# Expert weights: a casting DMA for w3, casts of w2 on ScalarE, two staging tiles for w1

## What is computed

```python
expert_weights, token_indices = jax.lax.top_k(expert_probs, cap)      # cap = 256 of 2048 tokens
expert_inputs = jax.vmap(lambda h, i: h[i])(hidden_states, token_indices)
gate = jax.nn.silu(jnp.einsum('becd,edf->becf', expert_inputs, w1))   # w1: (16, 1024, 2048) f32
value = jnp.einsum('becd,edf->becf', expert_inputs, w2)               # w2: (16, 1024, 2048) f32
expert_out = jnp.einsum('becf,efd->becd', gate * value, w3)           # w3: (16, 2048, 1024) f32
weighted = expert_out * expert_weights[..., None]                     # then scatter-added to tokens
```

## Time and profile before

| | us |
|---|---|
| median of two timed executions (6585.3 and 6603.8) | 6594.55 |
| the profiled execution, its own time | 6640.32 |
| its span on the slowest core (6) | 6638.7 |
| spans of the other cores | 6535.8 to 6595.6 |
| expert stage in it, first load to last y product | 3661 to 6111 |

### The profile page before, as it was taken

How to read it: one execution, slowest core, us unless ns; L and a number is a source line. 1 busy time by engine, 2 the same in 40 slices (tenths; PEclk the granted TensorE clock), 3 DMA queues, 4 the chain that set the end, 5 groups by cost and what they waited for, 6 DMA issues and landing times.

```text
span 6638.7 us, 53086 instructions; the slowest of 8 cores (6535.8 to 6638.7 us)
## 1 busy us (share of the span) xinstructions
PE 2939.7 (44%) x16857; PEld 1796.4 (27%) x16857; DVE 2005.4 (30%) x5175; ACT 879.9 (13%) x1731; POOL 169.8 (3%) x278
## 2 busy tenths in 40 slices
PE   0016263535353535744200455554554555455565
PEld 0004141323231323431000233433333333333222
DVE  1112131312221222224146233333333333233434
ACT  0004141415040404330000000000000000000000
POOL 0000000000000000000000000000000000000000
PEclk9977576767666766777555767777777777778888
DMA  1220101010101010013100554455565555453001
GB/s 45 58 58 4 51 4 51 5 50 6 49 5 49 5 49 5 10 62 106 38 9 1 177 167 156 152 165 163 170 177 161 174 171 168 158 165 111 32 32 35
DMA packets 387412, 541.05 MB, mean 82 GB/s; under 512 B 184100, under 2 KB 200774, under 8 KB 387142
## 3 DMA queue, kind: packets, MB, share of 16 engines
q1 hardware_dynamic: 263590, 235.36, 12.6%
q10 hardware_dynamic: 84992, 167.79, 8.1%
q0 software_dynamic: 38560, 134.51, 6.3%
HBM read 474.67 MB, written 29.36 MB: 76 GB/s over the span
## 4 chain that ended last, share of the span: by engine, by line
PE 33%; DMA 25%; DVE 17%; SPq 15%; issue 6%; DVEq 2%; ACT 2%; ACTq 0%; POOL 0%; POOLq 0%
DMA s_wf<-w 18%; SPq L85 15%; PE pO L521 8%; PE pO L1083 4%; PE pS L1165 4%; DMA s_otT<-s_otil 3%; DVEq L74 2%; PE pO L978 2%; DVE s_w3c L950 2%; PE pQ L404 2%; PE pQ L528 2%; DVE s_m L803 1%; PE pA L404 1%; PE pA L528 1%; DVE s_ohs L1153 1%
## 5 line engine op out<-in xcount | busy, mean ns | idle before, releaser
L521 PE MATMUL pO<-s_v,s_et 128*128 128x257 bf16 x4096 | 664.9, 298 | 424.5 <-ACT s_et L512 396.2
L521 PEld LDWEIGHTS pO<-s_v,s_et 128*128 128x128 bf16 x4096 | 432.1, 106 | 638.3 <-issue 517.5
L404 PE MATMUL pQ<-s_xnT,s_wqT 128*128 128x512 bf16 x256 | 80.6, 485 | 1093.9 <-DVE s_qt L412 722.7
L1054 PE MATMUL pQ<-s_xgT,s_w2c 128*128 128x256 bf16 x1024 | 224.2, 410 | 631.5 <-ACT s_gs L1047 631.5
L1083 PE MATMUL pO<-s_w3c,s_hb 128*128 128x512 bf16 x1024 | 344.1, 511 | 342.4 <-DVE s_hb L1072 342.4
L950 DVE CAST s_w3c<-s_wf 128x1024 bf16<-128x1024 f32 x256 | 177.6, 694 | 758.7 <-DMA s_wf<-w 574.8
L512 ACT ACTIVATE s_et<-pQ,s_bias 128x512 bf16<-128x512 f32 x512 | 338.5, 689 | 89.8 <-PE pQ L498 59.2
L1047 ACT ACTIVATE s_gs<-pQ 128x256 bf16<-128x256 f32 x128 | 42.2, 381 | 2289.6 <-DVE s_w2c L950 2269.2
L512 ACT ACTIVATE s_et<-pA,s_bias 128x512 bf16<-128x512 f32 x512 | 340.5, 691 | 27.6 <-PE pA L528 13.9
L404 PEld LDWEIGHTS pQ<-s_xnT,s_wqT 128*128 128x128 bf16 x256 | 29.8, 119 | 1142.1 <-issue 1132.9
L1054 PEld LDWEIGHTS pQ<-s_xgT,s_w2c 128*128 128x128 bf16 x1024 | 140.5, 142 | 704.7 <-issue 647.8
(11 more groups left out here) (198 smaller groups left out, 4065.1 us busy)
## 6 DMA issues: line engine op xcount, KB each, us to landing
s_wf<-w ACTq DMA_DIRECT2D x256, 512.0 KB, 6.0
s_wf<-w SPq DMA_DIRECT2D x256, 512.0 KB, 5.2
s_wf<-w POOLq DMA_DIRECT2D x256, 512.0 KB, 5.5
s_xstage<-x SPq DMA_DIRECT2D x16, 512.0 KB, 3.7
s_wsf<-wq ACTq DMA_DIRECT2D x16, 512.0 KB, 4.1
s_wsf<-wk ACTq DMA_DIRECT2D x16, 512.0 KB, 3.7
s_wsf<-wv ACTq DMA_DIRECT2D x16, 512.0 KB, 3.7
s_wsf<-wo ACTq DMA_DIRECT2D x16, 512.0 KB, 3.8
```

The costliest lines, as they stand in the source:

```text
L404: ins = t.matmul(bank[:], wbuf[:, j * 256 + et * 128: j * 256 + et * 128 + 128], s_xnT[:, j * T + qc * 512: j * T + (qc + 1) * 512], start ...
L521: return t.matmul(pO[qt][:, 0:257], s_et[:, kt * 512 + qt * 128: kt * 512 + qt * 128 + 128], s_v[:, kt * 257:(kt + 1) * 257], start=(kt == ...
L1054: g_ins = t.matmul(fb[f][:, 0:256], s_w2c[par][:, j * 512 + f * 128: j * 512 + f * 128 + 128], s_xgT[:, j * 256:(j + 1) * 256], start=(j = ...
```

## The change

- w3: no staging tile and no cast on an engine. One DMA from GpSimd's queue brings the chunk's 2 MB of f32 and writes bf16 straight into `s_w3c[npar]`. It waits for the y products that last read this buffer; the y products wait for it directly.
- w1: two staging tiles, `s_wf1[0]` and `s_wf1[1]`, with a semaphore each, so two quarters are loaded at a time. VectorE still casts them.
- w2: one staging tile. ScalarE both issues the loads and casts them (`AF.Copy`). The first load of the next chunk stands ahead of this chunk's silu, the four casts and the other three loads behind it.
- The first chunk is filled in the same way, w1 and w3 first, then w2.

```diff
+    s_wf1 = [sb(f"s_wf1{i}", [128, 1024], F32) for i in range(2)]
+    s_wf2 = sb("s_wf2", [128, 1024], F32)
+    ds_f1 = [p.dma_sem("ds_f1a"), p.dma_sem("ds_f1b")]
+    ds_f2 = p.dma_sem("ds_f2b")
+    ds_w3 = [p.dma_sem("ds_w3a"), p.dma_sem("ds_w3b")]
...
+    def issue_w1(e, dffc, qtr):
+        buf = qtr % 2
+        p.need("y", stg1_free[buf])
+        p.dma("y", s_wf1[buf][:].rearrange("p (j q) -> p j q", j=2),
+              wsrc(1, e, dffc, qtr), ds_f1[buf])
+
+    def cast_w1(qtr, par):
+        buf = qtr % 2
+        p.need_dma("v", ds_f1[buf])
+        p.need("v", w_cons[par][1])
+        tok = p.prod("v", lambda v, qtr=qtr, par=par, buf=buf: v.tensor_copy(
+            s_w1c[par][:, qtr * 1024:(qtr + 1) * 1024], s_wf1[buf][:]))
+        stg1_free[buf] = tok
+        wcast[par][1] = tok
...
+    def issue_w2(e, dffc, qtr):
+        p.need("s", stg2_box[0])
+        p.dma("s", s_wf2[:].rearrange("p (j q) -> p j q", j=2),
+              wsrc(2, e, dffc, qtr), ds_f2)
+
+    def cast_w2(qtr, par):
+        p.need_dma("s", ds_f2)
+        p.need("s", w_cons[par][2])
+        tok = p.prod("s", lambda s, qtr=qtr, par=par: s.activation(
+            s_w2c[par][:, qtr * 1024:(qtr + 1) * 1024], s_wf2[:], AF.Copy))
+        stg2_box[0] = tok
+        wcast[par][2] = tok
+
+    def load_w3(e, dffc, par):
+        p.need("g", w_cons[par][3])
+        p.dma("g", s_w3c[par][:].rearrange("p (q n) -> p q n", q=4),
+              w3.ap()[e][dffc * 512:(dffc + 1) * 512, :].rearrange(
+                  "(q p) n -> p q n", p=128),
+              ds_w3[par])
+
+    load_w3(0, 0, 0)
     for _q in range(4):
-        emit_casts()
-        issue_quarter(0, 0, _q, 0)
+        issue_w1(0, 0, _q)
+        cast_w1(_q, 0)
+    for _q in range(4):
+        issue_w2(0, 0, _q)
+        cast_w2(_q, 0)
...
-            emit_casts()
             if nxt is not None:
-                for qq in range(4):
-                    issue_quarter(nxt[0], nxt[1], qq, npar)
-                    emit_casts()
+                ne, nd = nxt
+                load_w3(ne, nd, npar)
+                issue_w1(ne, nd, 0)
+                issue_w1(ne, nd, 1)
+                cast_w1(0, npar)
+                issue_w1(ne, nd, 2)
+                cast_w1(1, npar)
+                issue_w1(ne, nd, 3)
+                cast_w1(2, npar)
+                cast_w1(3, npar)
+                issue_w2(ne, nd, 0)
             p.need("t", wcast[par][1])
...
                     s_gs[:, f * 256:(f + 1) * 256], fb[f][:, 0:256], AF.Silu)))
+            if nxt is not None:
+                for qq in range(4):
+                    cast_w2(qq, npar)
+                    if qq < 3:
+                        issue_w2(nxt[0], nxt[1], qq + 1)
             p.need("t", *sil)
...
             p.need("t", thb)
-            p.need("t", wcast[par][3])
+            p.need_dma("t", ds_w3[par])
```

More of the change, by code:

```diff
@@ L220, in build_program @@
     ds_smt = p.dma_sem("ds_smt")
-    ds_f = {k: p.dma_sem(f"ds_f{k}") for k in (1, 2, 3)}
     ds_wr = p.dma_sem("ds_wr")
@@ L918, in build_program @@
     prev_tym = None
[L920 to L924, removed]
-    w_cons = [{1: None, 2: None, 3: None} for _ in range(2)]
[L926 to L953, removed]
-    for _q in range(4):
-        emit_casts()
-        issue_quarter(0, 0, _q, 0)
+    s_wf1 = [sb(f"s_wf1{i}", [128, 1024], F32) for i in range(2)]
@@ new lines, in build_program, with wsrc @@
+    s_wf2 = sb("s_wf2", [128, 1024], F32)
+    ds_f1 = [p.dma_sem("ds_f1a"), p.dma_sem("ds_f1b")]
+    ds_f2 = p.dma_sem("ds_f2b")
+    ds_w3 = [p.dma_sem("ds_w3a"), p.dma_sem("ds_w3b")]
+    stg1_free = [None, None]
+    stg2_free = None
+    wcast = [{1: None, 2: None} for _ in range(2)]
+    w_cons = [{1: None, 2: None, 3: None} for _ in range(2)]
+    def wsrc(k, e, dffc, qtr):
+        w = w1 if k == 1 else w2
+        return w.ap()[e][qtr * 256:(qtr + 1) * 256,
+                         dffc * 512:(dffc + 1) * 512].rearrange(
+            "(j p) q -> p j q", p=128)
@@ new lines, in build_program @@
+    stg2_box = [None]
+    def issue_w2(e, dffc, qtr):
[15 more added lines that the diff above has]
+              ds_w3[par])
```

## The result

The changed kernel takes 6353.7 us in the median against 6614.4 for the kernel before in the same comparison; the ratio is 0.9605 (95% interval 0.9571 to 0.964). (Ratios use only executions in which neither half of the chip ran at a lower granted clock; medians are of all executions.) It is faster, by about 261 us where 421 were forecast, and 6353.7 lies 9 us above the range. A second comparison gave 0.9686 (0.964 to 0.9732).

A forecast was written before the change was run, and what follows sets the result against it. Round trips in the expert stage were taken as the bound, silu waiting for w2's cast. Saved: 402 us over 15 experts, minus 2.5 in the last, plus 22 at the start, 421; 6594.55 - 421 = 6174 us, range 6010 to 6345.

The forecast's parts named there:

- What bounds the kernel: Expert stage: round trips, not a full engine; silu waits for VectorE's w2 cast, 152.9 us an expert.
- DVE casts: VectorE keeps 4 of 12 casts per chunk: nothing by itself, w1 rounds hidden, DVE busy 354 us less.
- rival C: ScalarE reloads its function table between silu and copy: 9 us an expert, 144 in all, 6318 us; chance 0.03.
- The landing L: Time for one 512 KB w2 quarter on ScalarE's queue to land: 5.3 us, bounds for the mean 3.8 and 7.7.
- p: One w2 round on ScalarE, landing plus cast plus gaps: 6.6 us, with 1.3 for cast and gaps.
- the prediction's own form: Whole kernel, us saved = 15 x (99.4 - 11p) + (70.1 - 11p) + 22; zero at p = 9.0.
- The first interval: First to second chunk's silu in an expert, quarter 0 already landed: 2.7 + 3p = 22.5 us.
- Boundary, start and end: Silu across experts 50.8 us instead of 69.5; start saves 22 us; last expert's three intervals cost 2.5 us more.
- A: Expert stage: w2 lands in 3.8 us and the products become the bound, 685 us saved, 5909 us; chance 0.09.
- B: Loads bound by their rate, intervals inside an expert stay, only the boundary falls: 302 us saved, 6293 us; chance 0.12.
- the main case: Likeliest case for w2 quarters in the expert stage: landing between 4.3 and 6.5 us; chance 0.65.
- D: w3's 2 MB load slows w2 quarters; no gain from 7.7 us landing, 6877 us at 9.3; chance 0.05.

The follow-up runs named there:

- w2_part_only: The kernel before with only the w2 part: ScalarE issues and casts w2, w1 and w3 through VectorE as before; ratio 0.9999 to the kernel before.
- no_w3: The changed kernel with w3 loaded only for the first two chunks, later chunks using stale weights; 6110 us in the profiled execution.
- no_w1: The changed kernel with w1 loaded and cast only for the first two chunks; 6142 us in the only execution.
- all_cast_dma: The changed kernel with each weight brought by one 2 MB casting DMA per chunk from GpSimd's queue, no staging or engine casts; 0.8648 of the kernel before, 5694 us.

## Why the prediction was wrong in size

- *What bounds the kernel.* Right in kind: rounds, not an engine. But the wait of the silu for w2's cast was read as the only chain. `w2_part_only` shows a second one of the same length, w3's rounds between the y products and VectorE's evictions, and the trace before has it as its critical chain; it was not priced, and only the w3 part of the change removed it. That the forecast didn't break on it is luck: the change happens to do both.
- *DVE casts.* Busy time fell from 2005.4 to 1663.1 us, 342, close to the 354 forecast. That w1's rounds are hidden was nearly right: a w1 quarter lands after 7.4 us in the median and up to 15.6, where 9.3 was taken as the worst, and y waited for L945 15 times, 49 us in the whole span on core 4.
- *w3.* Forecast to land in 4.6 to 18.4 us and to cost nothing on the path: 13.2 us in the median, 17.4 at most, and the y products never wait for it. What it costs it costs through w2.
- *The cast on ScalarE.* 1.056 us measured, 1.03 forecast.
- *The function table (rival C).* Out: the trace after has five table loads, one of them at L1075. The Trainium skill, "ScalarE: Activation LUTs", section "Table sets: the hidden batching unit", says that copy is in every set; the trace agrees, as the number of table loads is the same as before, five.
- *The landing L, the step that failed.* Forecast 5.3, so p = 6.6. Measured p = 29.35/4 = 7.34 from the second and third intervals, which leaves L = 6.2 with the cast and gap of 1.13 taken off, and 6.2 is also the mean landing of the loads in the three intervals. Taking 5.3 between a lone 4.1 and a crowded 6.0 treated the crowded row as an upper bound. That row was of three equal loads of 512 KB, 1.5 MB in all; the change puts 3.5 MB in flight together, and there a quarter takes 8.6 us. The shorter landings outside the burst (3.9) don't make up for it, as ScalarE can use them for one quarter at a time only. The three intervals were 11 us an expert too long by this, the boundary 1.6. `no_w3` and `no_w1` show the cause: with either neighbour gone L is 5.0 in the three intervals and they shrink by 13 and 15 us. By the prediction's own form p = 7.34 would give 15 x (99.4 - 80.7) + (70.1 - 80.7) + 22 = 292 us saved, 6303 us on the median of 6594.55 that was shown.
- *The first interval.* Forecast 22.5 with quarter 0 ahead, measured 27.5. The w3 load of the next chunk leaves just behind s_wrow, w1's pair a little later, so the three round trips that follow the first silu stand mostly in the burst. 3p + 2.7 = 27.5 gives p = 8.3 there.
- *Boundary, start and end.* 50.8 against 52.4, 22 against 19, +2.5 against +2.
- *Rivals.* A (the products as bound) is what `all_cast_dma` reached by another way. B said that loads are bound by their rate all through: no, the DMA share swings between 0.43 and 1.01 and the mean rate is not the limit; but in the burst it is, which B as stated and the main case both missed. D is this same mechanism: it needed a mean landing of 7.7 and got 6.2.
- *The 3.2 us beside rival A.* The Trainium skill, "DMA: Bandwidth & Descriptors", section "Anatomy of one DMA — SWDGE (gpsimd) path", gives that fit for loads that GpSimd issues, while the w2 loads leave from ScalarE. No w2 load here landed under 3.4 us.

Another part of the distance lies in the comparison: the same kernel gave 0.9605 and 0.9686 in the two of them, and the kernel before 6614.4 in the median of ten where two had given 6594.55. Whether the limit in the burst is the core's own DMA engines, full by the profile, or partly memory shared with the other cores, was not separated; all cores ran the same loads in every run.

## What to carry to other kernels

When loads and casts run in single-buffered rounds, look for every chain of rounds that ends at the same products: removing one of two equal ones gained nothing here, and the two parts alone (0.9976 and 0.9999) say nothing of both together (0.9704, and 0.9605 to 0.9686 with the w1 part). Follow the chain that ended last through one whole period, and not the waits of one engine only. Price a round trip by what else will be in flight beside it after the change, in bytes, and not by the median before. And a long load that nobody waits for beat a short one in a sequence here: loads of 21 us with a whole chunk of room gave 0.8648 where loads of 4.6 us, four in a row with a cast between, gave 0.9686 against the same runs of the kernel before.

## What the runs showed of the hardware

- A 512 KB load from HBM on ScalarE's queue took 3.4 us at best, 3.9 in the mean with nothing beside it on its core, 8.6 beside w3's 2 MB load and two w1 quarters. The Trainium skill, "DMA: Bandwidth & Descriptors", section "Anatomy of one DMA — SWDGE (gpsimd) path", has a fit for a single load issued by GpSimd (about 2.0 us plus the bytes over 436 GB/s); an estimate of 3.2 us for this size follows from it. That is near the best case here and says nothing of the crowd.
- Casting on the way cost the DMA engines hardly more time here than a plain load: GpSimd's queue took 6.3% of 6638.7 us before for 134.51 MB, nearly all plain, and 6.7% of 6344.3 us after for the same bytes read (the profile then counts the 67.39 MB written), 418 against 425 us of the 16 engines.
- GpSimd issued a casting load of 2 MB in 0.74 us with rows of 4 KB (w3 in the changed kernel), 0.88 with rows of 2 KB (w1 in `all_cast_dma`).
- In the long flight whose queues are shown, one packet of w3 (4 KB read, 2 KB written) held an engine for 183 ns and one of w2 for 98 (share x 16 x 9.1 us over the packets). While w2's 272 packets moved, w3 moved 349 and the two w1 loads 520. The Trainium skill, same page, section "Queues, rings and completion order", says that an engine takes turns between queues by packet, each of several descriptors; the numbers of packets are compatible with turns, but no run here isolates the rule, and halving w3's rows left the w2 loads of the three intervals at 6.18 us against 6.24.
